# A three-stage MetaFormer kernel: joined small units, a second normalisation on wide columns, and experts' outputs stored side by side

## The reference

```python
# 1 token mixer: normalise over channels (eps 1e-6), quantise in groups of 36
#   (block floating point, 8 bits), 3x3 convolution, add x
x1 = x + conv2d(bfp_quantize(layernorm(x)), bfp_quantize(weight), bias, padding=1)
# 2 second normalisation over channels (eps 1e-5); its pixels are the tokens
t = layernorm(x1)                                  # M = 50176 tokens of 64
# 3 gate: a graph attention over 262144 edges plus loops gives 16 numbers per token
h = t @ W_gat                                      # (M, 4 heads, 4 experts)
e = leaky_relu(a_src[src] + a_dst[dst], 0.2)       # per edge and head
agg = segment_sum(h[src] * softmax_over_dst(e))    # (M, 16)
scores = layernorm16(agg + b_gat).mean(heads)      # (M, 4); top 2, softmax -> g
# 4 four experts, weighed by the gates, added to x1
for ei in range(4):
    hh = gelu(t @ W1[ei] + b1[ei])                 # 64 -> 128
    out = out + g[..., ei, None] * (hh @ W2[ei] + b2[ei])   # 128 -> 64
return x1 + out
```

## Time and profile before

| what | value |
|---|---|
| median of 3 runs | 4632.99 us (4620.16 to 4638.48) |
| the profiled execution | 4624.48 us |
| its span, first to last instruction | 4622.7 us |
| PE busy over the span | 3777.4 us, 82% |
| DVE, POOL, ACT busy | 2780.3, 2755.1, 976.0 us |
| mean granted PE clock | 0.824 |
| DMA | 283.90 MB, mean 61 GB/s |

### The profile page before, as it was taken

The page is one execution under the profiler, slowest core; times in us unless marked ns, Lnnn a source line. Parts: engine busy times, 40 slices in busy tenths (PEclk is TensorE's granted clock), DMA queues, the critical chain, the costliest instruction groups (busy, mean ns, idle before and its releaser), DMA issues. The chain is left out here.

```text
span 4622.7 us, 65200 instructions
## 1 busy us (share of the span) xinstructions
PE 3777.4 (82%) x20605; PEld 2611.9 (57%) x20641; DVE 2780.3 (60%) x3739; ACT 976.0 (21%) x2569; POOL 2755.1 (60%) x2785
## 2 busy tenths in 40 slices
PE   4785323599864999999999999999999999861599
PEld 1453323477753666666666666666666666661122
DVE  7778999767744554445544555445544555447666
ACT  0110000000002333333333333333333333310000
POOL 2000888766643777777777777777777777771000
PEclk8898555788876888988888888988888888875699
DMA  1243111588864111211111111111111111171598
GB/s 48 58 97 85 45 50 41 64 109 98 106 101 83 36 36 33 39 32 36 36 36 33 35 36 36 36 32 35 36 36 32 36 36 36 30 10 2 151 290 248
DMA packets 320349, 283.90 MB, mean 61 GB/s; under 512 B 199554, under 2 KB 276098, under 8 KB 319748
## 3 DMA queue, kind: packets, MB, share of 16 engines
q1 hardware_dynamic: 213748, 202.06, 20.7%
q0 software_dynamic: 87936, 29.35, 9.6%
q10 hardware_dynamic: 18576, 51.39, 2.9%
HBM read 160.30 MB, written 122.27 MB: 61 GB/s over the span
## 5 line engine op out<-in xcount | busy, mean ns | idle before, releaser
L1079 POOL DMA_INDIRECT gath<-tab_d,src_no x2192 | 2068.3, 944 | 752.7 <-issue 667.7
L449 POOL DMA_INDIRECT edge_d<-run_slots,slots x544 | 658.2, 1210 | 667.3 <-ACT run_slots L639 506.7
L1212 PEld LDWEIGHTS C<-spread,lo_hot 128*128 128x128 f32 x4384 | 809.3, 243 | 307.4 <-issue 211.0
L1212 PE MATMUL C<-spread,lo_hot 128*128 128x160 f32 x4384 | 880.8, 369 | 116.1 <-DVE spread L1375 112.7
L1387 DVE TENSOR_TENSOR acc<-acc,C 128x160 f32 x1096 | 351.3, 321 | 911.8 <-PE C L1212 770.1
L1198 PEld LDWEIGHTS C<-dst_rows,lo_hot_t 128*128 128x128 f32 x4384 | 556.2, 206 | 92.0 <-issue 78.3
L1198 PE MATMUL C<-dst_rows,lo_hot_t 128*128 128x32 f32 x4384 | 573.3, 287 | 12.2 <-ACT lo_hot_t L1097 12.2
L1102 ACT ACTIVATE hid<-A,b1s 128x392 f32<-128x392 f32 x512 | 300.8, 588 | 1240.9 <-PE A L1221 1240.9
L1221 PE MATMUL A<-T,w1s 64*128 64x392 f32 x1024 | 532.2, 603 | 0.0
L560 PE MATMUL C<-wide_rec,hot_lo 128*128 128x136 f16 x2048 | 266.9, 305 | 297.8 <-DVE wide_rec L817 297.8
L1232 PE MATMUL A<-hid,w2s 128*64 128x392 f32 x1024 | 454.5, 526 | 0.0
(11 more groups left out here) (263 smaller groups left out, 3239.5 us busy)
## 6 DMA issues: line engine op xcount, KB each, us to landing
mlp_d<-mlp ACTq DMA_DIRECT2D x128, 392.0 KB, 2.4
mlp<-mlp_d SPq DMA_DIRECT2D x64, 784.0 KB, 4.6
gath<-tab_d,src_no POOLq DMA_INDIRECT x2192
pixels<-in_x SPq DMA_DIRECT2D x32, 392.0 KB, 8.3
src<-in_x SPq DMA_DIRECT2D x32, 392.0 KB, 9.5
T<-t_d SPq DMA_DIRECT2D x128, 98.0 KB
X<-x_d SPq DMA_DIRECT2D x64, 196.0 KB, 5.1
out<-X SPq DMA_DIRECT2D x128, 98.0 KB, 2.6
```

What stands on the lines that cost most here:

```text
L449: pool.indirect_dma_start(edge_d, bass.IndirectOffsetOnAxis(ap=slots[:, k, c:c + 1], axis=0), run_slots[:, k, c * RUN:(c + 1) * RUN, :].re ...
L1079: pool.indirect_dma_start(gath[:, g % BUFS, j, :], None, tab_d, bass.IndirectOffsetOnAxis(ap=src_no[:, t:t + 1], axis=0)).then_inc(gathere ...
L1212: mm = pe.matmul(C[:, bank, at:at + HI * VALS], lo_hot[:, k % UNROLL, u * U + j, :], spread[:, u * U + j].rearrange("p h v -> p (h v)"), s ...
```

## The change

Three edits.

1. **Image loop.** The variance is now made by 4 matmuls over 392 columns against `thin` (128x32, 1/64 in two columns), each to its own 32 partitions of one bank; ACT takes the root of 128x392, DVE the reciprocal of 128x392, and 4 matmuls against `fan`, each over 32 of the partitions, spread it. The multiplication is one operation. The sort's matmuls are cut into four parts of 16 and placed between the steps of the normalisation; the projection belongs to the same image and stands behind the convolution; `group_places` stands behind the multiplication; the one-hots of the second half are spread around the subtraction.
2. **Edge stage.** Each expert's output is taken out of PSUM on the 64 partitions of its half, with four 64x392 operations per half chunk in place of two of 128x392; `mlp_d` holds the four experts of a partition side by side.
3. **Last stage.** The gates are spread for both halves at once (4 matmuls of 24x128 and 392 columns per step into four banks, A and C in turn), DVE multiplies 128x1568 once and adds the products in pairs (128x784), POOL adds the two sums and then x1. The folding matmuls are gone. Of the gates a second copy, shifted by half an image, is loaded on 12 more partitions, by two more DMAs.

The constants `thin`, `fan` and a larger `pick` are made by POOL at the start.

```diff
@@ PE, image loop
                         pe.wait_ge(s["summed"], b + 1)
                         mean_of(pe, X[k], s["mean2_ready"])
-                        if not (isinstance(b, int) and b == 0):
-                            project(b - 1, 1 - k)
+                        if sorts:
+                            sort_step(g, 1 - k, 0, 0)
                         pe.wait_ge(s["squared2"], b + 1)
-                        variance_of(pe, k, s["var2_ready"])
-                        if not (last and k == 1):
-                            sort_step(g, 1 - k, 0)
+                        for c in range(CHUNKS):
+                            mm = pe.matmul(A[c * QUAD:(c + 1) * QUAD, 0, 0:CHUNK], thin[:], S[:, c, :], start=True, stop=True)
+                        mm.then_inc(s["var2_ready"], 1)
+                        if sorts:
+                            sort_step(g, 1 - k, 0, 1)
                         pe.wait_ge(s["rstd2_ready"], b + 1)
-                        spread_rstd(pe, A, s["rstd2_spread"])
+                        for c in range(CHUNKS):
+                            mm = pe.matmul(A[:, c, 0:CHUNK], fan[c * QUAD:(c + 1) * QUAD, :], std2[c * QUAD:(c + 1) * QUAD, :], start=True, stop=True)
+                        mm.then_inc(s["rstd2_spread"], 1)
+                        if sorts:
+                            sort_step(g, 1 - k, 1, 0)
                         pe.wait_ge(s["tokens_ready"], b + 1)
-                        if not (last and k == 1):
+                        if sorts:
                             convolve(i + k, 1 - k)
-                            sort_step(g, 1 - k, 1)
+                            sort_step(g, 1 - k, 1, 1)
+                        project(b, k)
@@ DVE, image loop
                             spread_step(*at, 0)
+                            one_hot_step(*at, 1, 0)
...
                         dve.tensor_tensor(D[k], X[k], A[:, :, 0:CHUNK], ALU.subtract).then_inc(s["centred2"], 1)
                         if sorts:
+                            one_hot_step(*at, 1, 1)
+                            spread_step(*at, 1)
+                        dve.wait_ge(s["deviated2"], b + 1)
+                        dve.reciprocal(std2[:], std2[:]).then_inc(s["rstd2_ready"], 1)
+                        dve.wait_ge(s["rstd2_spread"], b + 1)
+                        dve.tensor_tensor(D[k], D[k], A[:, :, 0:CHUNK], ALU.mult).then_inc(s["tokens_ready"], 1)
+                        if sorts:
                             group_places(*at)
-                        dve.wait_ge(s["deviated2"], b + 1)
-                        dve.reciprocal(rstd[:], dev[:]).then_inc(s["rstd2_ready"], 1)
-                        if sorts:
-                            one_hot_step(*at, 1)
-                            spread_step(*at, 1)
-                        dve.wait_ge(s["rstd2_spread"], b + 1)
-                        scale(D[k], A, s["tokens_ready"])
@@ edge stage, PE
                 def down(m, h, e):
...
-                    if e % 2 == 0 and not (isinstance(m, int) and m == 0 and h == 0 and e == 0):
-                        pe.wait_ge(s["pair_out"], v * 2 + e // 2)
+                    if not (isinstance(m, int) and m == 0 and h == 0 and e == 0):
+                        pe.wait_ge(s["expert_out"], v)
+                    pe.matmul(A[h * CH:(h + 1) * CH, 3, 0:CHUNK], w2s[:, e, :], hid[:], start=True, stop=True).then_inc(s["expert_done"], 1)
@@ last stage
+                def spread_gates(r, t, first):
...
+                    if t >= 2 or not first:
+                        pe.wait_ge(s["gated_ready"], r * STEPS + t - 1)
+                    for e in range(EXPERTS):
+                        mm = pe.matmul(gates_of(t)[:, e], pick[:, e, :], gate_t[:, t // PER].rearrange("e q l -> e (q l)")[:, n:n + CHUNK], start=True, stop=True)
+                    mm.then_inc(s["gate_ready"], 1)
...
+                def add_up(r, t, first):
...
+                    hold(pool, s["paired"], n + 1, s["pool_turns3"])
+                    pool.tensor_tensor(four[:, t % 2], pairs[:, t % 2, 0], pairs[:, t % 2, 1], ALU.add).then_inc(s["added"], 1)
+                    pool.wait_ge(s["added"], n + 1)
+                    pool.tensor_tensor(X1[:, t % NBUF], X1[:, t % NBUF], four[:, t % 2], ALU.add).then_inc(s["summed3"], 1)
...
+                def weigh_and_pair(r, t, first):
...
+                    dve.wait_ge(s["gate_ready"], n + 1)
+                    if t >= 2 or not first:
+                        dve.wait_ge(s["paired"], n - 1)
+                        dve.wait_ge(s["added"], n - 1)
+                    dve.tensor_tensor(gated[:, t % 2], mlp[:, t % NBUF], gates_of(t), ALU.mult).then_inc(s["gated_ready"], 1)
+                    dve.wait_ge(s["gated_ready"], n + 1)
+                    dve.tensor_tensor(pairs[:, t % 2], gated[:, t % 2, 0:2], gated[:, t % 2, 2:4], ALU.add).then_inc(s["paired"], 1)
```

More of the change, by code:

```diff
@@ L186, in build @@
         w2s = sb("w2s", [P, EXPERTS, CH])
-        b2s = sb("b2s", [P, 2])
-        pick = sb("pick", [3 * EXPERTS, EXPERTS, CH], BF16)
+        b2s = sb("b2s", [P, EXPERTS])
+        pick = sb("pick", [2 * 3 * EXPERTS, EXPERTS, P], BF16)
         fold = sb("fold", [P, CH])
+        thin = sb("thin", [P, QUAD])
+        fan = sb("fan", [P, P])
         A = ctx.enter_context(nc.psum_tensor("A", [P, 4, 512], F32))
@@ L420, in _ @@
                     link(pool, pool.memset(halves[h * CH:(h + 1) * CH, h * CH:(h + 1) * CH], 1.0 / CH), step)
+                link(pool, pool.memset(thin[:], 0.0), step)
+                for h in range(2):
+                    link(pool, pool.memset(thin[h * CH:(h + 1) * CH, h:h + 1], 1.0 / CH), step)
+                link(pool, pool.memset(fan[:], 0.0), step)
+                for c in range(CHUNKS):
+                    for h in range(2):
+                        link(pool, pool.affine_select(out=fan[:, h * CH:(h + 1) * CH], in_=fan[:, h * CH:(h + 1) * CH], compare_op=ALU.not_equal, fill=1.0,
+                                                      base=-(c * QUAD + h), pattern=[[0, CH]], channel_multiplier=1), step)
                 link(pool, pool.memset(eps_c[:], 1e-6), step)
@@ L432, in _ @@
                 link(pool, pool.memset(pick[:], 0.0), step)
-                for r in range(3):
-                    link(pool, pool.affine_select(out=pick[:], in_=pick[:], compare_op=ALU.not_equal, fill=1.0, base=-r * EXPERTS,
-                                                  pattern=[[-1, EXPERTS], [0, CH]], channel_multiplier=1), step)
+                for h in range(2):
+                    mine = pick[:, :, h * CH:(h + 1) * CH]
+                    for r in range(3):
+                        link(pool, pool.affine_select(out=mine, in_=mine, compare_op=ALU.not_equal, fill=1.0, base=-(h * 3 + r) * EXPERTS,
+                                                      pattern=[[-1, EXPERTS], [0, CH]], channel_multiplier=1), step)
                 pool.memset(scratch_i[:], 0).then_inc(s["const_ready"], 1)
@@ L797, in take, with one_hot_step @@
                                         C[:, h * 2:h * 2 + 2, :].rearrange("p k n -> p (k n)")).then_inc(s["ranks_taken"], 1)
-                def one_hot_step(i, k, j):
+                def one_hot_step(i, k, j, which=None):
                     g = i * 2 + k
-                    if not (isinstance(g, int) and g == 0):
+                    if which != 1 and not (isinstance(g, int) and g == 0):
                         dve.wait_ge(s["step_sums"], g * 2 + j - 1)
@@ L1541, in fold_pair @@
-                def fold_pair(r, t, h, j, first):
-                    w = (t * 2 + h) * 2 + j
-                    if h == 0 and j == 0 and (t >= 2 or not first):
-                        pe.wait_ge(s["summed3"], r * STEPS + t - 1)
-                    pe.wait_ge(s["gated_ready"], r * STEPS * 4 + w + 1)
-                    pe.matmul(C[h * CH:(h + 1) * CH, t % 2, 0:CHUNK], fold[:], gated[:, w % 4, :],
-                              start=(j == 0), stop=(j == 1)).then_inc(s["folded"], 1)
-                def round_of(r, first):
-                    todo = [(t, h, j) for t in range(STEPS) for h in range(2) for j in range(2)]
-                    for w, at in enumerate(todo):
-                        spread_gates(r, *at, first)
-                        if w >= 2:
-                            fold_pair(r, *todo[w - 2], first)
-                    for at in todo[-2:]:
-                        fold_pair(r, *at, first)
@@ new lines, in _ @@
+                for t in range(STEPS):
+                    spread_gates(0, t, True)
+                with pe.Fori(1, ROUNDS) as r:
+                    for t in range(STEPS):
+                        spread_gates(r, t, False)
+            @block.gpsimd
+            def _(pool):
+                def add_up(r, t, first):
+                    n = r * STEPS + t
+                    hold(pool, s["paired"], n + 1, s["pool_turns3"])
+                    pool.tensor_tensor(four[:, t % 2], pairs[:, t % 2, 0], pairs[:, t % 2, 1], ALU.add).then_inc(s["added"], 1)
```

(12 more changed lines are left out.)

134 lines of the change are left out of this document (61 added, 73 removed).

## The result

| | before | after |
|---|---|---|
| median, same chip | 4629.4 us (4 runs) | 4510.2 us (4502.8 to 4522.3, 4 runs) |
| ratio | | 0.9745, 95% interval 0.9714 to 0.9776 |
| profiled span | 4622.7 us | 4501.1 us |
| mean turn of the image loop | 31.1 us | 27.0 us |
| length of the gathers, first to last start | 2735.0 us | 2735.2 us |

The kernel is 2.5% faster, 119 us; 60 were forecast, and 4510 lies under the range. Both stages that were to gain gained more.

A forecast was written before the change was run, and what follows sets the result against it. It took the image loop as a PE, DVE and ACT chain, the edge stage as paced by POOL's gathers, the last stage by PE. Terms -24 + 0 - 36 = -60 gave a median of 4573 us, range 4524 to 4616.

The forecast's parts named there:

- The turn at full clock: Image loop: one turn built step by step at full clock falls from 28.2 to 26.4 us, 15 turns giving 27.
- I leave the 2.8 us of lower clock as they are but book 24: Image loop: lower-clock loss per turn kept unchanged; gain booked as 24 us, since the clock may fall oftener.
- So some 2.8 us a turn are the lower clock: Image loop before the change: mean turn 31.1 us against 28.2 at full clock, the difference laid to the clock.
- Rival 3: More than forecast: DMA follows to 3.3 us a step and image-loop clock stays up (-62, -45), 4526 us; chance 0.08.
- the DMA's price of a step: Last stage: transfers taken as the latest limit, 3.55 us plus 0.15 for gates, 3.7 a step against 4.29.
- a step in which the two can't run together: Last stage: if POOL's additions can't run beside DVE's pair addition, a step is 2.3 + 0.97 + 0.2 = 3.4 us.
- the edge stage (0): Edge stage: added ACT operations and waits stay hidden behind POOL's gathers; booked 0, ends -1 and +13 us.
- POOL's addition: Last stage: each of POOL's two 128x392 additions taken as 1.0 us, two and their waits 2.3.
- the start of the last stage: Last stage: the first product waits for two more gate transfers, costing 1.5 us.
- The end: Last stage: two POOL additions replace one fold and one addition at the end, costing about 1 us.
- the turn of 29 to 30 us: Sign in the profile after: image-loop convolutions on average 29 to 30 us apart.
- the last stage of some 245 us: Sign in the profile after: last stage some 245 us long, DVE and POOL waiting, mostly for DMA.

The follow-up runs named there:

- The filled kernels: Matmuls without use put into PE's image-loop waits: kernel before 4600.8 us; new order with narrow columns 4553.0; changed kernel 4486.7 to 4504.6.
- The 2x2 of order and columns: Changed kernel with old or new image-loop order, narrow or wide variance and spread: old narrow 4565.3 us, old wide 4569.7, new narrow 4578.2, new wide 4510.2.
- e6: Changed kernel with POOL's two last-stage additions cut from 392 to 8 columns: 4509.1 us, ratio 0.9727.
- e7: Changed kernel with the experts' outputs stored and loaded as float16, products and sums still float32: 4486.3 us, ratio 0.9690.

## Why the prediction was wrong

**The turn at full clock was right.** I built 26.4 us at full clock; with the clock held at 0.98 the mean is 26.2, and the median 25.9, lower by what `thin` and `fan` had been booked too high. Its parts: reciprocal 2.60 for 2.61, multiplication 1.79 for 1.8, `thin` 0.87 for 1.0, `fan` 0.94 for 1.4; from the start of the subtraction to that of the reciprocal 5.6 (1169.04 to 1174.65, in the changed kernel) for 5.7. The gain of 2.0 a turn is 30 of the 61 us.

**The step that failed** is "I leave the 2.8 us of lower clock as they are but book 24". It took the low clock for a tax on every turn that any edit leaves in place or raises. The granted clock did fall a little, as that sentence feared (0.84 to 0.82). But its price depends on what stands behind PE's waits and whether that is on the chain. The chain of the old turn held the convolution, which lost 1.7 us, and the narrow variance, which lost 2.3; the new one is DVE's from end to end, a slow convolution lies beside `group_places`, and only `thin` and `fan` are left on it, which lose 0.7 each where they are slow. Measured: 2.9 before, 0.8 after, so 31 us more in 15 turns. Of these 6 lie in the first turn (36.4 against 30.1 us), whose wait for a scatter is not the clock's; the reading "So some 2.8 us a turn are the lower clock" had overlooked it, and 2.5 is what the other turns show. The filled kernels show the term itself, though only 1.1 of it could be given back to the kernel before. The 2x2 of order and columns shows that both edits are needed for the gain. Rival 3, which had "the clock stays up since wide matmuls replace those after which it fell", came nearer for the loop (-45, measured -61) with the wrong ground: the clock did not stay up.

**The second mis-sized term** is the DMA's price of a step, "halfway between 3.0 and the 4.15", 3.55, and 0.15 for the gates: 3.7. It was 3.40, near the low bound. The binding limit was named rightly (`e6`, `e7`), the number wrongly: 4.64 MB in 16 us was read as what the transfers can do, though PE paced the stage then; now 348 GB/s flow over the whole stage. 63 x 0.3 is 19 of the 20 us that the last stage gained over the forecast. (Halfway between the two is 3.58 and not 3.55, a slip of 2 us over the stage.)

The Trainium skill (SBUF — State Buffer, Who interferes with whom) says that a DVE instruction with two SBUF inputs contends with a POOL instruction that reads SBUF, and calls the port pair that they share an exclusive lock. Here the pair addition took 1236 ns beside POOL's additions and 975 beside additions of 8 columns, and with half the bytes it ended as if it had hardly begun before POOL was done, so this case agrees. The prediction had 3.4 for a step in which the two can't run together. The measured step was 3.40 too, but by luck: it was DVE's 3.03 with DMA waits of 0.36, and where the transfers were out of the way (`e7`) that case cost 3.11.

**Right** were the edge stage (0), POOL's addition (1.0 booked, 1.01 measured), DVE's product (1.79), and the start of the last stage (1.5 booked, 0.9). The end cost 3.0 where 1 was booked. Of the signs named, the reciprocal right behind DVE's fields, POOL's additions and the gathers came as said; the turn of 29 to 30 us and the last stage of some 245 us (227) did not.

## What to carry to other kernels

The low clock isn't a rate by which a stage's time is multiplied: list which units run at it and whether they are on the chain, and build the turn once at full clock and once with each unit behind a PE wait slow. An edit that moves PE's waits and one that shortens what stands behind them can each gain nothing alone and much together, so test them together. When a stage is not paced by its DMAs, their share and rate in it are no measure of what they can carry; the bound that is nearest is a stretch where they alone are late.

## What the runs showed of the hardware that was not expected

- Added matmuls without use made a kernel faster: with 13 of 384 columns per turn in the kernel before, the mean turn fell from 31.1 to 30.0 us (ratio 0.9941, 0.9925 to 0.9957).
- A DVE addition of 128x784 with both inputs in SBUF that began 0.54 us before the end of one of POOL's took 1.38 us in place of 0.98; POOL's kept its 1.01.
- ACT took 582 ns for 64x392 and 587 for 128x392: half the partitions save nothing.
- Four float32 matmuls of 392 columns onto 32 partitions each took 0.87 us, four from 32 partitions each 0.94, at the upper level, against 2.8 to 2.9 for four of 128x128.
- The kernel before took 1.4 times as long on one chip as on the others, and there edits that are free elsewhere cost 108 us in the edge stage. Why stays open.
